# Four first loads with a semaphore each, another order in SyncE's queue, and the identity first on ScalarE

## What is computed

```python
qkv = x @ qkv_w + qkv_b                      # self attention, 16 heads of 16
q, k, v = split(qkv); q, k = rotary(q), rotary(k)
attn = softmax(q k^T * 16**-0.5) v
x = layernorm(x + attn @ out_w + out_b)
Q, K, V = x WQ + bQ, ctx WK + bK, ctx WV + bV  # cross attention, 16 heads of 64
allowed = causal and (key position < length of the batch)
x = layernorm(x + softmax(where(allowed, Q K^T / 8, -1e6)) V @ WO + bO)
e = argmax(x @ router_w)                     # 14 experts, one for each token
x = layernorm(x + softmax(x @ router_w)[e] * (gelu(x w1[e] + b1[e]) w2[e] + b2[e]))
```

## Time and profile before

| what | value |
|---|---|
| time, 3 runs | 512.77 us median (511.94, 512.77, 515.41) |
| time of the profiled execution | 515.03 us |
| its span, first to last instruction | 513.3 us |
| PE busy | 466.4 us, 91% of the span |
| DVE, ACT, POOL busy | 67%, 60%, 42% |

### The profile page before, as it was taken

How to read it: one execution, slowest core, us unless ns; L and a number is a source line. 1 busy time by engine, 2 the same in 40 slices (tenths; PEclk the granted TensorE clock), 3 DMA queues, 4 the chain that set the end, 5 groups by cost and what they waited for, 6 DMA issues and landing times.

```text
span 513.3 us, 12715 instructions
## 1 busy us (share of the span) xinstructions
PE 466.4 (91%) x4461; PEld 400.7 (78%) x4461; DVE 345.9 (67%) x967; ACT 308.9 (60%) x1404; POOL 217.1 (42%) x299
## 2 busy tenths in 40 slices
PE   3687799998999999999999999989999998899991
PEld 2375587886877988878878978878889887899981
DVE  2779648856769767897578597685366636665653
ACT  2366647776768877877468585776475683333340
POOL 1365424462435544553236246543143432254443
PEclk9879789999999999999999999999999998999997
DMA  5762124435141323543151414060151393699900
GB/s 163 198 156 69 45 93 149 183 115 180 33 170 58 121 85 127 184 128 155 43 178 32 172 33 175 20 216 10 37 169 49 90 349 124 179 378 373 358 31 17
DMA packets 43804, 69.83 MB, mean 136 GB/s; under 512 B 12297, under 2 KB 33914, under 8 KB 43021
## 3 DMA queue, kind: packets, MB, share of 16 engines
q1 hardware_dynamic: 40344, 39.81, 24.8%
q10 hardware_dynamic: 926, 25.83, 13.5%
q0 software_dynamic: 2464, 3.31, 2.1%
HBM read 59.08 MB, written 29.77 MB: 173 GB/s over the span
## 4 chain that ended last, share of the span: by engine, by line
PE 71%; DVE 14%; DMA 6%; issue 3%; ACT 3%; POOL 2%; SPq 1%; DVEq 0%; POOLq 0%; ACTq 0%
PE bank L1418 26%; PE bank L1635 8%; PE bank L1492 7%; PE bank L1830 5%; PE bank L1819 5%; PE bank L1624 5%; PE bank L1664 4%; PE bank L1656 2%; PE bank L1601 2%; DMA vX<-v_tile 2%; DMA out_bias<-in_L_attn_out_b_dram 2%; ACT probs L1094 2%; DVE qk L1200 2%; PE bank L1451 2%; DVE rot L1198 2%
## 5 line engine op out<-in xcount | busy, mean ns | idle before, releaser
L1094 ACT ACTIVATE probs<-bank,neg_max 100x100 f32<-100x100 f32 x512 | 170.1, 369 | 35.6 <-DVE neg_max L1230 27.2
L996 POOL TENSOR_TENSOR probs<-probs,row_inv 100x400 f32<-100x400 f32 x128 | 112.7, 901 | 105.3 <-DVE row_inv L1235 105.1
L1094 ACT ACTIVATION_READ_ACCUMULATOR probs<-bank,neg_max 100x1 f32 x512 | 118.0, 230 | 0.0
L1230 DVE TENSOR_REDUCE neg_max<-bank 100x4 f32<-100x400 f32 x128 | 68.6, 564 | 10.8 <-PE bank L1624 5.4
L1635 PE MATMUL bank<-ident,probs 100*100 100x100 f32 x512 | 68.3, 256 | 6.3 <-POOL probs L996 4.6
L1635 PEld LDWEIGHTS bank<-ident,probs 100*100 100x100 f32 x512 | 51.0, 130 | 18.2 <-POOL probs L996 6.6
L1103 ACT COPY probsT<-bank 100x400 f32<-100x400 f32 x62 | 30.8, 496 | 42.5 <-PE bank L1635 36.5
L1242 DVE COPY probsT<-bank 100x400 f32<-100x400 f32 x66 | 37.6, 570 | 23.0 <-PE bank L1635 17.3
L1418 PE MATMUL bank<-cT_h,W_K 128*128 128x250 f32 (+1 forms) x224 | 46.6, 293 | 4.3 <-DVE kX L1157 1.7
L1492 PE MATMUL bank<-yT,W_Q 128*128 128x250 f32 (+1 forms) x224 | 50.1, 366 | 0.0
L1418 PE MATMUL bank<-W_O,oX_h 128*125 128x256 f32 (+1 forms) x224 | 43.8, 296 | 0.7 <-DVE oX_l L1252 0.7
(11 more groups left out here) (185 smaller groups left out, 964.9 us busy)
## 6 DMA issues: line engine op xcount, KB each, us to landing
expert_rows<-c_empty ACTq DMA_DIRECT2D x13, 1935.0 KB, 8.8
w<-in_L_ffn_w_dram SPq DMA_DIRECT2D x36, 512.0 KB, 7.3
vX<-v_tile SPq DMA_DIRECT2D x14, 200.0 KB
vX<-v_tile SPq DMA_DIRECT2D x12, 150.0 KB
xs<-in_x_dram SPq DMA_DIRECT2D x12, 125.0 KB
vX<-v_tile SPq DMA_DIRECT2D x12, 100.0 KB
kX<-in_L_xattn_WK_dram SPq DMA_DIRECT2D x2, 512.0 KB, 9.8
qX<-in_L_xattn_WV_dram SPq DMA_DIRECT2D x2, 512.0 KB, 6.4
```

What stands on the lines that cost most here:

```text
L996: probs_ready.mark(pool.tensor_tensor(v, v, r, ALU.mult), step)
L1094: i = act.activation(probs[:, k % SLOTS, w], sc_bank[p % 2 * 2 + u][0:T, w], ACT.Exp, bias=neg_max[:, k % SLOTS, h:h + 1], accum_out=row_s ...
L1230: max_ready.mark(dve.tensor_reduce(neg_max[:, k % SLOTS, :], src, AX_X, ALU.max, negate=True), step)
```

## The change

Each of the four small loads gets a semaphore of its own, and each step waits for the one it needs: `v_out` and `qk_out` for `qkv_bias`, `rot` for `rotary`, `keys_p` and `keys_v` for `own`, `bias.s` for `out_bias`. In SP's queue `qkv_bias` and `rotary` move ahead of tile 1 of x, and `out_bias` moves behind the first context tile. On ACT the load of `ident` is started before that of `len_row`. The diff:

```diff
--- before.py
+++ after.py
@@ -568,7 +568,10 @@
 
 
             ident_in = sem("ident_in")
-            small_in = sem("small_in")
+            qkv_bias_in = sem("qkv_bias_in")
+            rotary_in = sem("rotary_in")
+            own_in = sem("own_in")
+            out_bias_in = sem("out_bias_in")
             late_in = sem("late_in")
             lens_in = sem("lens_in")
             lens_wide_in = sem("lens_wide_in")
@@ -793,7 +796,6 @@
             def raw_there(k):
                 return raw_in[k], 16 * len(weight_pieces[k][3])
 
-            N_SMALL = 4 * 16
             N_KV = 16
             N_ROUTE = 10 * 16
             N_LATE = 5 * 16
@@ -835,13 +837,12 @@
                 load_x(0)
                 for k in range(2):
                     load_piece(k)
+                sp.dma_start(qkv_bias[:, :], qkv_b.rearrange("(o n) -> o n", o=1).broadcast_to([TT, 3 * D])).then_inc(qkv_bias_in, 16)
+                sp.dma_start(rotary[:, :, :].rearrange("p j w -> p (j w)"), c_rotary).then_inc(rotary_in, 16)
                 load_x(1)
-                for dst, src in (
-                    (qkv_bias[:, :], qkv_b.rearrange("(o n) -> o n", o=1).broadcast_to([TT, 3 * D])), (rotary[:, :, :].rearrange("p j w -> p (j w)"), c_rotary),
-                    (own[:, :], c_own), (out_bias[:, :], out_b.rearrange("(o n) -> o n", o=1).broadcast_to([TT, D])),
-                ):
-                    sp.dma_start(dst, src).then_inc(small_in, 16)
+                sp.dma_start(own[:, :], c_own).then_inc(own_in, 16)
                 load_c(0)
+                sp.dma_start(out_bias[:, :], out_b.rearrange("(o n) -> o n", o=1).broadcast_to([TT, D])).then_inc(out_bias_in, 16)
                 load_x(2)
                 for k in (3, 4):
                     load_piece(k)
@@ -968,7 +969,7 @@
                     elif kind == "bias":
 
                         if step[1] == "s":
-                            wait(small_in, N_SMALL)
+                            wait(out_bias_in, 16)
                             wait(*projected.at(("xT", n)))
                             t, a = xs[0:size(n), n % XS, :], out_bias
                         else:
@@ -981,7 +982,7 @@
                         make_hot(pool, wait, n, (0,), biased, step)
                     elif kind == "keys_p":
 
-                        wait(small_in, N_SMALL)
+                        wait(own_in, 16)
                         for t in tiles_of(n):
                             wait(*taken(("qkT", t)))
                         if n >= 2:
@@ -1026,8 +1027,8 @@
                 wait = Waits(act)
 
 
+                act.dma_start(ident[:, :], c_ident).then_inc(ident_in, 16)
                 act.dma_start(len_row[:, :], lens.rearrange("(o n) -> o n", o=1)).then_inc(lens_in, 16)
-                act.dma_start(ident[:, :], c_ident).then_inc(ident_in, 16)
                 def empty(j):
                     chunk = rows.rearrange("(e j r) w -> e j (r w)", e=NE + 1, r=P)[:, j, :]
                     act.dma_start(chunk, c_empty.rearrange("(o r) w -> o (r w)", o=1).broadcast_to([NE + 1, P * ROW])).then_inc(emptied[j // 2], 16)
@@ -1175,7 +1176,7 @@
                                                                  scalar=len_f[:, n:n + 1], in1=later_twice_sb[:, :, :],
                                                                  op0=ALU.is_ge, op1=ALU.max), step)
                     elif kind == "qk_out":
-                        wait(small_in, N_SMALL)
+                        wait(qkv_bias_in, 16)
                         wait(*projected.at(("qk", n)))
                         if n:
                             wait(*rot_ready.at(("rot_sum", n - 1)))
@@ -1190,6 +1191,7 @@
                             t = rotary[0:w, n % (RT // TT), k * half:(k + 1) * half]
                             return t.unsqueeze(1).broadcast_to([w, 2 * H, half])
 
+                        wait(rotary_in, 16)
                         wait(*took.at(("qk_out", n)))
                         if n:
 
```

## The result

| | before | after |
|---|---|---|
| median of 22 runs | 512.03 us (509.15 to 515.41) | 513.95 us (510.36 to 516.99) |
| ratio | | 1.0038, 95% interval 1.0020 to 1.0056 |
| profiled execution, its span | 515.03 us, 513.3 us | 512.55 us, 510.8 us |

The changed kernel is slower by 1.9 us (1.0 to 2.9 by the interval). The forecast was +0.9, a small loss within 1%. That the forecast's 513.7 us lies so near 513.95 is in part luck: it was built on the median of three runs before, 512.77, and the 22 runs give 512.03. The profiled execution of after is one of its quick ones, quicker than that of before; so the two spans can't be subtracted, and what follows compares places.

A forecast was written before the change was run, and what follows sets the result against it. It took the start as bound by the wait for out_bias, then one chain of engines passing any shift to the end whole; -1.58 + 2.45 = +0.9 us on 512.8 gave 513.7 us, range 510.8 to 517.0.

The forecast's parts named there:

- Part 2: Tile 1 of x behind qkv_bias and rotary on five DMA engines: xT.1 at 11.4 us, bounds 10.4 and 12.0.
- Part 3: PE's walk from xT.1 through v.0 and v.1: qk.0 starts at 15.0 us against 14.14, +0.9 us.
- Part 1: v_out.0 on DVE no longer waits for out_bias: alone worth up to 1.58 us; qkv_bias is next late.
- rival A: At the first loads, tile 1 of x is not late: -2.1 us, 510.7 us; chance 0.1.
- Part 4: Identity issued first on ACT: xT.0 starts about 0.5 us earlier, hidden before tile 1 lands, so 0.
- Part 5: len_row loaded second, behind the identity: W_K issued some 0.4 us later, within 3.1 us of slack, so 0.
- The sum: Gap closed at the start, -1.58 us, plus late tile 1, +2.45 us: +0.9 us in all.
- B: PE's clock comes up earlier, before qk.0, and the low stretch may end earlier: 512.0 us; chance 0.2.
- C: PE's clock stays low longer, past 31.4 us into later products and scores: 516.4 us; chance 0.12.

The follow-up runs named there:

- x1_moved_only: The kernel before, shared semaphore kept, with only tile 1 of x moved behind qkv_bias and rotary; ratio 1.0043 to the kernel before.
- x1_back: The changed kernel with tile 1 of x moved back ahead of qkv_bias and rotary; ratio to the kernel before 1.0000, and 0.9983 when repeated.
- bias_128_after: The changed kernel with qkv_bias and out_bias loaded to 128 partitions instead of 125; ratio 0.9963 to the kernel before.
- sems_only: The kernel before with the four semaphores alone and no load moved; ratio 1.0001 to the kernel before.
- bias_128_again: Repeat of the changed kernel with tile 1 of x ahead of qkv_bias again and both biases at 128 partitions; ratio 0.9956 to the kernel before.
- after_warm: The changed kernel with 20 transposes of the identity on PE while it waits for tile 1 of x; ratio 1.0002 to the kernel before.

## Why the prediction was right, and where its steps were off

- *Part 2, tile 1 goes behind `qkv_bias` and `rotary` on five engines:* right, and the cause of the loss (`x1_moved_only` has it by this alone, `x1_back` is without it, `bias_128_after` turns it into a gain). Its size was off: I took 11.4 us for xT.1 and 12.0 as the upper bound; the traces gave 11.92, 12.11 and 12.66. The upper bound was the end of one stretch in one trace; it left nothing for how much this landing scatters from one execution to the next, 0.7 us here. The lower bound took 145 GB/s for 448,000 bytes, 3.1 us; xT.1 came 4.6 us later than before, which is 97 GB/s, and the half microsecond shown above had 92.
- *Part 3, the walk to qk.0:* the order was right, the length was not. From xT.1 to qk.0 I added 0.68 + 2.85 + waits = 3.6 us; measured 3.01 (11.92 to 14.93), 3.03 and 3.04. In the trace of after v.0 begins 0.34 us after xT.1 begins, while the second transpose still runs; I had put the two end to end. And v.0 to qk.0 is 2.67 us from start to start, not 2.85, since qk.0 begins before the last product of v.1 has ended. This error and that of part 2 have opposite signs, so it is in part luck that 15.0 us was forecast for qk.0 and 14.93 to 15.70 measured.
- *Part 1, what goes with the wait for `out_bias`:* I priced the closed gap at 1.58 us (it is 2.18 in the second trace of before) and named `qkv_bias` as next late. With tile 1 in front, DVE does wait for `qkv_bias`, 1.7 to 2.3 us in `x1_back`, `x1_back_again` and `sems_only`, but PE loses at most 0.46 us by it before qk.0. What I left out stands behind: tile 2 of x and W_K. DVE has qk.0 3.3 us or more earlier than before, and 2.1 us of that are left at 98 us, but `sems_only` brought 1.0001 and `x1_back` 1.0000 and 0.9983. The 1.58 us are just outside the interval of `sems_only` (0.9970 is -1.5 us) and inside that of `x1_back_again` (-2.4 us). So a shift of the start was not shown to reach the end whole, as I had taken it to, and where the rest of this gain goes stays open. By the measured times the price of rival A, 2.1 us, was too large too.
- *Part 4, the identity:* hidden, as said; xT.0 started at 4.29, 4.61 and 5.01 us, against 5.94 and 5.43 before, rather more than the 0.5 us forecast, and no ratio shows it. The idle time of PE before xT.1 was given as about 4 us, which doesn't follow from the places forecast (from 5.4 + 0.7 to 11.4 is 5.3); it was 6.98.
- *Part 5, `len_row`:* POOL marked the first check at 4.71 instead of 2.72, and W_K was still issued at 7.63, no later than the 7.97 before. No cost, as said.
- *The sum:* +0.9 forecast, +1.9 measured (1.0 to 2.9). The mean place of qk.0 gives +1.1. The rest isn't settled: three traces scatter by 0.7 us at xT.1 alone, by 2.2 us at the K product, since the clock rises at another place each time, and by 2.6 us more between qk_out.5 and qk_out.6.
- *Rivals B and C* aren't outcomes of their own but what one execution or the other gets: in the first trace of the changed kernel the products of qk.0 took 0.40 us (B), in the second and third 0.63 but for the last one of the third. For C, a low stretch that by itself makes the difference, there is no run; the fall of the clock near 130 us has its size, but it comes in the kernel before as well.

## What to carry to other kernels

A finer semaphore is worth what stands behind the next latest load, so look at all of the loads that land within a microsecond or two of the one waited for, before counting a gap as gain. A load moved ahead of another in one queue, on the same engines, is paid by that other: here 437 KB moved ahead of tile 1 made it 4.6 us later. So ask what the engine with the strictest order needs first, even if the step it is asked for isn't the one that is late. And count the rows of a load: here 125 rows ran on five DMA engines, and rounding two broadcasts up to 128 was worth about 0.7 to 0.8% in the changed kernel (0.9963 against 1.0030 to 1.0044), more than the reordering had put at stake.

## What the runs showed of the hardware that I had not expected

- A 128-row load can come late by the 125-row loads ahead of it. W_K, issued near 8 us in all of these kernels, let ACT start at 16.96 in `x1_back_again`, with 125-row biases ahead of it, and at 14.69 in `bias_128_again`, with 128-row ones.
- Twenty transposes in a row, 4.47 us of them, ending 3.09 us before the next work, did not bring the clock up for that work: its 128x512 products took 0.63 us, as without them. They ran at the lower level themselves, at 0.22 us each (four transposes in a row take 1.03 us at the lower level, at 27.96 us in `x1_back_again`, and 0.62 at the upper, at 21.52 in the changed kernel). In `x1_back`, where PE went from xT.1 at 7.43 to the end of qk.0 with one gap of 0.15 us, the last product of qk.0 took 0.40 us; in `sems_only`, with one gap of 1.02 us, 0.39. The Trainium skill (TensorE: Matmul & The Clock Gate, section on the clock gate) says that idleness takes the clock back down; `after_warm` can't show it, since its clock was not up before the 3.09 us of idleness.
- Executions of one kernel spread over 6 us (509.15 to 515.41) while v_out.0 stood at 13.66 and 13.76 in its two traces. What differs later on is above all at which products the clock is up. The largest single piece lies between qk_out.5 and qk_out.6: 36.7 to 37.5 us in the seven traces where the clock granted from 120 to 136 us is 1.00, 38.8 to 40.6 in the seven where it is 0.79 to 0.89.
